# Softmax weights transposed and stored two tasks at a time, loads moved to the sync engine, and one row minimum taken inside an addition

## The reference

```python
x = x + 0.5 * ffn(layernorm(x), Wg, Wu, Wd)      # part A
x = x + attention(layernorm(x), w_q, w_k, w_v, w_o, rel_emb)
x = x + 0.5 * ffn(layernorm(x), Wg, Wu, Wd)      # part B, the same weights
```

## Time and profile before

| What | us |
|---|---|
| three runs of the kernel, median (lowest to highest) | 1436.86 (1435.93 to 1439.6) |
| the profiled execution, its own time | 1438.3 |
| its span, first to last instruction | 1436.5 |
| mean granted TensorE clock, share of full speed | 0.994 |

### The profile page before, as it was taken

The page is one execution under the profiler, slowest core; times in us unless marked ns, Lnnn a source line. Parts: engine busy times, 40 slices in busy tenths (PEclk is TensorE's granted clock), DMA queues, the critical chain, the costliest instruction groups (busy, mean ns, idle before and its releaser), DMA issues.

```text
span 1436.5 us, 29572 instructions
## 1 busy us (share of the span) xinstructions
PE 1375.4 (96%) x8632; PEld 1076.9 (75%) x8632; DVE 1278.3 (89%) x2541; ACT 1101.9 (77%) x2642; POOL 1087.4 (76%) x956
## 2 busy tenths in 40 slices
PE   8999999999999999999999999999999999999898
PEld 7787676777777777777777778777777777778686
DVE  6887898999999999999999989899999999899565
ACT  6656778878778887788888878778887778788454
POOL 7967787787778877887778768787777877677555
PEclk9999999999999999999999999999999999999999
DMA  6404999999999999999999999899999999897200
GB/s 185 142 15 125 154 192 187 178 204 170 180 188 175 165 178 176 187 160 189 164 152 209 170 167 179 148 191 177 171 172 161 192 162 173 161 173 142 44 1 8
DMA packets 718386, 225.08 MB, mean 157 GB/s; under 512 B 652305, under 2 KB 697745, under 8 KB 718225
## 3 DMA queue, kind: packets, MB, share of 16 engines
q1 hardware_dynamic: 556224, 172.45, 72.9%
q10 hardware_dynamic: 162000, 50.75, 19.4%
HBM read 60.95 MB, written 69.86 MB: 91 GB/s over the span
## 4 chain that ended last, share of the span: by engine, by line
PE 47%; DVE 19%; ACT 9%; issue 7%; DMA 6%; ACTq 4%; SPq 4%; POOL 3%; POOLq 0%; DVEq 0%
PE work L708 9%; PE work L710 9%; PE work L709 9%; PE acc L786 5%; PE acc L787 4%; DVE hid L1071 4%; PE acc L791 4%; DMA probs_t<-probs 4%; DVE hid L1065 3%; DVE negmax L1167 3%; ACTq L1000 3%; PE work L839 3%; DVE work L1162 3%; ACT work L960 2%; DVE probs L1176 2%
## 5 line engine op out<-in xcount | busy, mean ns | idle before, releaser
L1218 POOL TENSOR_TENSOR hid_lo<-hid,hid_hi 128x512 fp32r<-128x512 f32 x512 | 663.5, 1302 | 215.6 <-ACT hid_hi L915 115.1
L909 ACT ACTIVATE hid<-work 128x512 f32<-128x512 f32 x512 | 310.1, 606 | 123.9 <-PE work L710 84.9
L1065 DVE SCALAR_TENSOR_TENSOR hid<-hid,work 128x512 f32<-128x512 f32 x512 | 345.7, 680 | 53.9 <-ACT hid L909 53.4
L1071 DVE TENSOR_TENSOR hid<-hid,work 128x512 f32<-128x512 f32 x512 | 346.6, 680 | 33.6 <-PE work L710 31.2
L915 ACT CAST hid_hi<-hid 128x512 fp32r<-128x512 f32 x512 | 320.1, 630 | 49.7 <-DVE hid L1071 30.8
L786 PE MATMUL acc<-hid_hi,wd 128*128 128x512 f32 x512 | 216.5, 423 | 12.4 <-ACT hid_hi L915 9.9
L1167 DVE TENSOR_REDUCE negmax<-work 128x1 f32<-128x384 f32 (+3 forms) x352 | 219.2, 634 | 1.2
L1233 POOL TENSOR_TENSOR probs<-exps,probs 128x512 f16<-128x512 f32 (+1 forms) x160 | 172.0, 1075 | 62.8 <-ACT probs L972 59.8
L708 PE MATMUL work<-xt,wg 128*128 128x512 f32 x512 | 207.0, 404 | 5.4 <-DVE xt L1040 1.5
L708 PE MATMUL work<-xt,wu 128*128 128x512 f32 x512 | 206.1, 402 | 2.8 <-DVE hid L1071 1.9
L791 PE MATMUL acc<-hid_lo,wd 128*128 128x512 f32 x512 | 204.1, 401 | 1.0 <-POOL hid_lo L1218 0.7
(11 more groups left out here) (97 smaller groups left out, 2184.5 us busy)
## 6 DMA issues: line engine op xcount, KB each, us to landing
prob_window_scratch<-probs SPq DMA_DIRECT2D x384, 80.0 KB, 3.5
rel_win<-rel_window_scratch ACTq DMA_DIRECT2D x250, 96.0 KB, 4.3
q_scratch<-rope SPq DMA_DIRECT2D x16, 512.0 KB, 4.2
qq<-q_scratch ACTq DMA_DIRECT2D x32, 256.0 KB
rel_window_scratch<-g_s SPq DMA_DIRECT2D x32, 256.0 KB, 5.1
k_scratch<-rope SPq DMA_DIRECT2D x16, 512.0 KB, 4.2
kk<-k_scratch ACTq DMA_DIRECT2D x32, 256.0 KB
prob_window_scratch<-probs SPq DMA_DIRECT2D x32, 256.0 KB, 3.2
```

What stands on the lines that cost most here:

```text
L909: act.activation(hid[:, arg % HB, :], work[bank_of["gate", arg]][:, :], ACT.Tanh, scale=0.5).then_inc(s_tanh, 1)
L1065: dve.scalar_tensor_tensor(out=hid[:, arg % HB, :], in0=hid[:, arg % HB, :], scalar=1.0, in1=work[bank_of["gate", arg]][:, :], op0=ALU.add ...
L1071: dve.tensor_tensor(hid[:, arg % HB, :], hid[:, arg % HB, :], work[bank_of["up", arg]][:, :], ALU.mult).then_inc(s_hid, 1)
L1218: pool.tensor_tensor(hid_lo[:, arg % 2, :], hid[:, arg % HB, :], hid_hi[:, arg % 2, :].bitcast(F32), ALU.subtract).then_inc(s_hlo, 1)
```

## The change

1. **Pairs.** The tasks of tiles 1, 2 and 3 go by twos into one place: per group one single (tile 0) and five pairs, GP = 6. `p_turn` and `store_band` are issued once a pair, 192 times each; `part_of` places high and low parts so that both heads of a pair lie together. PB goes from 4 places of tasks to 3 of pairs, TB from 6 of tasks to 3 of pairs (twice as wide).
2. **Loads.** `load_q`, `load_k`, `load_window` and `load_band` are issued on SP's queue, with the same waits.
3. **Tiles 2 and 3.** `largest` runs first, over the columns without the window, into far; `near` then adds the window and takes the minimum in one instruction, with far as its start.
4. **Tile 0's scores** are one matmul of 512 columns: q stands, and the keys padded by head (`q_pad` made from kk) move.
5. **Buffers and order.** XB goes from 5 to 4, v_s becomes a part of rope, so `project` of the next batch waits for `v_split` and `v_add` for the store of k; the band's table is laid out for pairs of heads. `PASSES`, the due times (the first two batches get 144 units each) and `LATER` are new.

```diff
-    XB = 5
+    XB = 4
-    TB = 6
-    PB = 4
+    TB = 3
+    PB = 3
-    PASSES = (("A", 0), ("A", 1), ("A", 2), ("A", 3), ("B", 0), ("A", 4), ("B", 1), ("A", 5), ("B", 2),
-              ("A", 6), ("B", 3), ("A", 7), ("B", 4), ("B", 5), ("B", 6), ("B", 7))
-    UNITS_FROM, UNITS_TO = 146, 1406
+    PASSES = (("A", 0), ("A", 1), ("A", 2), ("A", 3), ("B", 0), ("B", 1), ("A", 4), ("A", 5), ("B", 2),
+              ("B", 3), ("A", 6), ("A", 7), ("B", 4), ("B", 5), ("B", 6), ("B", 7))
+    UNITS_FROM, UNITS_TO = 144, 1404
...
+    GP = (GK + 1) // 2
+    def pair_of(k):
+        return k // GK * GP + (k % GK + 1) // 2
+    def pair(m):
+        k = m // GP * GK + 2 * (m % GP)
+        return range(k - 1 if m % GP else k, k + 1)
...
+        def part_of(k, part):
+            _, i, places, keys = task(k)
+            cols = len(places) * keys
+            place = probs[:, pair_of(k) % PB, :]
+            if i == 0:
+                return place[:, 0:2 * cols].rearrange("p (b h c) -> p b h c", b=2, h=2)[:, :, part, :]
+            at = places[0] * cols + part * cols if i == 1 else places[0] % 2 * cols + part * 2 * cols
+            return place[:, at:at + cols]
...
                 if name == "store_band":
-                    sp.wait_ge(*lower_part(arg))
+                    for k in pair(arg):
+                        sp.wait_ge(*lower_part(k))
...
+                    sp.dma_start(bass.AP(pwin_t, (quad % (2 * NT) * HQ + places[0]) * 2 * TILE + lo,
+                                         [[W, P], [TILE, n], [1, W - lo]]), near).then_inc(stored(arg)[0], 16)
                 if name == "p_turn":
-                    blocks = 2 * len(places) * (i + 1)
+                    blocks = rows_of(arg) * (i + 1)
...
+                if name == "load_window":
+                    gg, i = arg // NT, arg % NT
+                    sp.wait_ge(s_gst, 16 * (gg + 1))
+                    if arg >= WB:
+                        sp.wait_ge(s_near, last_of(arg - WB) + 1)
...
                 if name == "scores":
-                    for n, a in enumerate(places):
-                        done = pe.matmul(bank[:, n * keys:(n + 1) * keys], q_pad[:, quad % 2, a, :],
-                                         kk[:, gg % 2, 0:keys], start=True, stop=True)
+                    if i == 0:
+                        pe.wait_ge(s_qld[gg % 2], 16 * (gg // 2 + 1))
+                        done = pe.matmul(bank[:, :], qq[:, gg % 2, 0:P], q_pad[:, quad % 2, :, :].rearrange(
+                            "p a k -> p (a k)"), start=True, stop=True)
...
                 if name == "near":
+                    if i < 2:
+                        dve.tensor_tensor(near, near, window_of, ALU.add).then_inc(s_near, 1)
+                    else:
+                        dve.wait_ge(s_max, arg + 1)
+                        dve.tensor_tensor_reduce(out=near[:, :, 0], in0=near[:, :, 0], in1=window_of[:, :, 0],
+                                                 op0=ALU.add, op1=ALU.min, scale=1.0, scalar=far[:, arg % 4:arg % 4 + 1],
+                                                 accum_out=negmax[:, place:place + 1]).then_inc(s_near, 1)
                 if name == "largest":
+                    if i < 2:
+                        dve.wait_ge(s_near, arg + 1)
+                        dve.tensor_reduce(negmax[:, place:place + len(places)], heads, AX.X, ALU.min).then_inc(s_max, 1)
+                    else:
+                        dve.wait_ge(s_sc, arg + 1)
+                        dve.tensor_reduce(far[:, arg % 4:arg % 4 + 1], heads[:, 0, 0:i * P - R], AX.X, ALU.min).then_inc(s_max, 1)
```

More of the change, by code:

```diff
@@ L280, in macaron_kernel @@
                 step("DVE", wide(columns), due[k] + 2, "p_lo", k, ("p_hi", k))
-            step("SP", 1.5 if columns == L else 1.25, due[k] + 2, "p_turn", k, lower(k),
-                 ("values", values_of(quad_of(k - TB)) if k >= TB else None), ("split_lo", (E - 1, 2)), lands=LATE)
-            step("SP", 1.2 if HEADS[i] == 2 else 0.62, due[k] + 2.5, "store_band", k, lower(k),
-                 ("load_band", back(quad, 2 * NT)), lands=LATE)
+        for m in range(GP * HG * t, GP * HG * (t + 1)):
+            k = pair(m)[-1]
+            done = [lower(x) for x in pair(m)]
+            step("SP", 1.6, due[k] + 2, "p_turn", m, *done,
+                 ("values", values_of(quad_of(pair(m - TB)[-1])) if m >= TB else None), ("split_lo", (E - 1, 2)), lands=LATE)
+            step("SP", 0.55, due[k] + 2.5, "store_band", m, *done,
+                 ("load_band", back(quad_of(k), 2 * NT)), lands=LATE)
     for p, (kind, t) in enumerate(PASSES):
@@ L564, in exp_of, with by_heads, rows_of, turned_probs @@
             return exps[:, lents_to[k] % EB, :] if lent(k) else work[bank_of["scores", k]]
-        def turned_probs(k):
-            return probs_t[:, k % TB, :].bitcast(F16).rearrange("p (b q) -> p b q", q=P)
+        def by_heads(k, ap):
+            _, i, places, keys = task(k)
+            columns = ap[:, 0:len(places) * keys]
+            return columns.rearrange("p (b c) -> p b c", b=2) if i == 0 else columns
+        def part_of(k, part):
+            _, i, places, keys = task(k)
+            cols = len(places) * keys
[4 more added lines that the diff above has]
+            return place[:, at:at + cols]
+        def rows_of(m):
+            return 2 * sum(HEADS[TASKS[k % NK][1]] for k in pair(m))
+        def turned_probs(m):
+            return probs_t[:, m % TB, :].bitcast(F16).rearrange("p (b q) -> p b q", q=P)
+        def block_of(i, a, part, j):
+            return ((a // 2 * 2 * (i < 2) + part) * 2 + a % 2) * (i + 1) + j
         def parts(v):
@@ L844, in _ @@
                     t, g = gg // HG, gg % HG
-                    for k in range(first_of(NT * gg + tiles[0]), last_of(NT * gg + tiles[-1]) + 1):
-                        pe.wait_ge(*turned(k))
+                    for m in range(pair_of(first_of(NT * gg + tiles[0])), pair_of(last_of(NT * gg + tiles[-1])) + 1):
+                        pe.wait_ge(*turned(m))
                     if arg == 0:
@@ L1172, in _ @@
+                if name in ("near", "largest") and lent(arg) and name == ("largest" if i < 2 else "near"):
+                    dve.wait_ge(s_max if i < 2 else s_near, arg + 1)
+                    dve.tensor_scalar(shifted[:, place:place + len(places)], negmax[:, place:place + len(places)],
+                                      math.log(SCALE), None, ALU.add).then_inc(s_shifted, 1)
                 if name == "p_lo":
-                    quad, i, places, keys = task(arg)
-                    cols = len(places) * keys
```

259 lines of the change are left out of this document (119 added, 140 removed).

## The result

The changed kernel takes 1446.45 us (median of 5 runs, 1442.68 to 1447.49) against 1435.93 us of the kernel before in the same session (1433.27 to 1439.6). The ratio is 1.0073, with a 95% interval from 1.0053 to 1.0093: it is slower by 0.7%. 1417 us were forecast, and the range ended at 1446.

A forecast was written before the change was run, and what follows sets the result against it. It took TensorE (96% busy) and VectorE (89%) as near full in attention, each briefly awaiting the other. From 1436.9 us, gains of 6, 5 and 14 less 5 for SP's queue gave 1417 us, range 1396 to 1446.

The forecast's parts named there:

- SP's queue: SP's issuing: fewer transposes and stores balance the added loads, 0 change in load; 5 us added back for changed order.
- The mechanism that the text named for SP: Attention on SP's queue: a load over about 10 us late stops VectorE's window sum, then hid_hi and TensorE.
- the terms of the sum: Whole kernel: 6 us from VectorE, 5 from TensorE, 14 from ScalarE's queue, less 5 for SP: 20 us less.
- ScalarE's queue: Loads leaving ScalarE's queue: 237 us of issuing go, a quarter of its 57 us on the chain gained, 14 us.
- VectorE: Tiles 2 and 3, shorter reductions and window sum fused with minimum: 27 us less work, 6 us of time.
- TensorE: Tile 0's scores as one matmul of 512 columns: 10 us less of TensorE's stream, 5 us of time.
- The transfers: DMA transfers in the attention stage: same bytes and packets, one queue at 91% barely fits, 0 us.
- the third rival: SP's ring in the attention stage: one queue becomes the bound, decided at 26.5 ns a packet; 1460 us, chance 0.18.
- the signs that the text gave for trouble: Late window sums, band or values matmuls waiting over 10 us, transposes landing over 7 us, one queue at 95% or more.
- its milder forms: SP's ring becoming the bound less severely: 1442 to 1450 us, a third of a chance of 0.18.
- Order: Passes 5 to 10, buffers and the newly laid order: no instruction added, 0 us with 8 us either way.

The follow-up runs named there:

- e13: Changed kernel with each of its 192 probability transposes turning only the first half of its blocks, same order (output incomplete): 1409.2 us.
- e14: Kernel before with the same halving of its 352 probability transposes, same order (output incomplete): 1426.7 us.
- e15: Changed kernel with only the 128 band loads issued on ScalarE's queue again, same order: 1431.9 us.
- e3: Changed kernel with window sum and minimum over all columns as two plain instructions again in tiles 2 and 3, same order: 1444.2 us.
- e12: Changed kernel with tile 0's scores as four matmuls of 128 columns again, same order: 1443.9 us.
- e17: Changed kernel with band, q and k loads on ScalarE's queue again, only the 253 window loads staying on SP's, same order: 1436.0 us.
- e1: Changed kernel with all loads of q, k, windows and bands on ScalarE's queue again, same order: 1479.5 us.
- e4: Kernel before with its window, q, k and band loads moved to SP's queue, in its own order: 1515.6 us.
- e2: Changed kernel with two transposes of half the blocks in place of each pair's one, same order: 1475.6 us.
- e11: Changed kernel with all due times of the attention two units later, order laid anew: 1453.1 us.
- e16: Kernel before with all due times of the attention two units later, order laid anew: 1455.8 us.
- e5: Kernel before with only the changed kernel's order of passes, order laid anew: 1475.8 us.
- e6: Changed kernel with the old order of passes, five x buffers and three places of hid, order laid anew: 1458.8 us.
- e7: Changed kernel with three places of hid instead of four, order laid anew: 1483.6 us.
- e8: Changed kernel with passes B 2 and A 6 one earlier, A 5 and B 3 one later, four x buffers: 1465.4 us.
- e10: Changed kernel with old passes, five x buffers, four places of hid, one buffer for cosine and sine, and even due times: 1470.3 us.

## Why the prediction was wrong, step by step

**SP's queue: the step that failed.** The text took 1.63 us for a transpose of 16 blocks, "as band_t has", and found "no change in load, 0". Two things are wrong in that row. band_t has 8 blocks, not 16 (L413 of the kernel before: 4 tiles by 2 parts of 128 columns), so it has the size of the transposes that go away and says nothing of a doubled one. And it was read by its median, where its mean is 2.09. In the changed kernel the 96 transposes of 16 blocks take 3.56 us in the mean, and all 192 take 2.63, 505 us instead of 313. The band loads take 0.70 us each instead of 0.37, 42 us more; the other loads 213 us where 190 were taken. SP's issuing rose by 135 us instead of falling by 13. The whole was booked at 5 us against the change; e13 against e14 shows 29 us between the kernels (37 - 8), e15 shows 14.5 us for the band loads alone. The mechanism that the text named for SP (a late window stops VectorE) was not it either: the window loads land in 2.6 us now, and no window sum waits for one. The values and band matmuls stood still, which the text called covered because they wait for a tile's last task anyway. That left out that their transposes stand in SP's queue behind the others.

With both kernels' transposes halved, the changed one is 17.6 us ahead (1426.7 to 1409.2), near the 20 that were forecast. That does not bear out the terms of the sum: e3 and e12 find nothing for two of them, and where the 17.6 come from is open.

**ScalarE's queue.** Booked at 14 us gain, a quarter of its 4% of the chain. The queue did leave the chain, but e15 and e17 show that 192 of the 445 loads cost nothing on ScalarE in the new order, so taking them off gave nothing there. Only the windows cost, 43 us in the new order (e1 against e17). In the order of the kernel before, moving the loads off costs 81 us (e4). So what a load costs on either queue depends on the order in which it stands; that each order fits its own queues is the likely reason, and is not shown.

**VectorE.** The forecast was 27 us less work and 6 us of time. The busy time gives 11 us less (e3 against the changed kernel), the time nothing. The reductions were right (383 and 516 ns for 389 and 518). The sum with minimum is 500 ns, as taken, and then a read of the accumulator of 141 ns, which was not in the sum and in part overlaps. By the busy time the form costs some 120 ns more than the plain sum (165 less for a reduction, of which 43 stay), where 59 were taken. The rule cited from the Trainium skill (VectorE: DVE Perf Modes, Two Vector instructions with no wait between them), that such an instruction is two, agrees with the trace: 256 reads stand in it, at 141 ns. Taking it into the sum would have mended the work, not the time.

**TensorE.** 10 us of the stream and 5 us of time were forecast. Busy time differs by 3 us between e12 and the changed kernel, the time not at all. That TensorE is busy 11 us less than before looks like the forecast, but e12 puts only 3 of it down to this term.

**The transfers.** The packets take 25.1 ns each (0.975 x 144 x 16 / 89,357), under the 26.5 ns at which the third rival said that one queue would be full. By that measure the rival did not happen. But the measure is a poor one: in e13, the fastest run, a packet takes 27.0 ns (0.815 x 144 x 16 / 69,575). Of the signs that the text gave for trouble, two came: 97.5% in one queue, and band and values matmuls that wait for transfers by more than 10 us. Two did not: transposes land in 4.6 us at the median (4.5 before), not over 7, and no window sum waits. So the rival had the sign and the place (SP's ring), and its milder forms, 1442 to 1450, hold the measured time; its price, 1460 us, was 14 too high (and its 92 us for 28.5 ns should be 90). What the runs show is the time that SP needs to issue: in e2 it grows and the ring takes the same bytes, for 29 us, and in e1 the transposes stay slow with the loads in another ring. That the ring costs something as well is not ruled out. The rule cited with it from the Trainium skill (DMA: Bandwidth & Descriptors, Queues, rings and completion order) would let one expect that loads land later behind transposes. This trace does not show that: the windows land in 2.6 us at the median instead of the 4.3 of the earlier trace rows. Landing counts from the issue, and what grew is the time in front of it.

**Order.** It was booked at 0 with 8 us either way. e11 and e16 show 7 and 21 us for a shift of two units. Both moved to the slow side, but two shifts give no rule. The term wanted some 20 us of width; its 8 us came from no row.

**Open.** The price of the order of passes. e5 and e6 against e7 say 25 to 41 us, e8 to e10 say nothing or the reverse, and e11 and e16 say that such differences can come from the laying alone. Why a transpose of 16 blocks takes twice as long to issue as one of 8 or 12, and up to 5.8 us, was not shown; it does so with the loads gone (3.51 us in the mean in e1). How much of the 10.5 us is the lower clock behind the waits, up to 16 us by the estimate above, and how much the waits themselves. And whether the transposes cost by their issuing alone or by their bytes too.

## What to carry to other kernels

Before a queue gets more DMAs, sum what it issues by means, not medians, and compare the sum with the span: SP was at 899 of some 1200 us before anything was added. Here means alone would not have been enough: 192 x 2.09 for the transposes, with stores and loads as they were (98 and 245 us by means), is 744 us, still less than the 767 of the transposes and stores before. What was missing is one row of a transpose of the new size. Check that the row you borrow has the size of the thing you price; if none has, try one before the sum. When a package moves one queue's load to another, try the pieces one at a time in the order as it stands: the band loads alone were worth 14.5 us.

## What the runs showed that was not expected

- A DMA transpose on SP's queue takes 1.65 us to issue in the mean with 8 blocks, 1.74 with 12 and 3.56 with 16 (before: 1.40 with 6, 1.68 with 8). One of 12 is nearly as cheap as one of 8; one of 16 costs as much as two of 8.
- Moving 445 loads from ScalarE's to SP's queue in an unchanged order costs 81 us; moving 253 of them the other way in the other order costs 43.
- A shift of due times by 2 of 1536 units, with the same work, moves a kernel of 1435 us by 21 us.
- One place less of hid (three instead of four), order laid anew, comes with 37 us (e7), from which the effect of the new laying (7 and 21 us in e11 and e16) is not parted.
